# A transformer block on one core: fp8 rounding placed behind the second split, and the first batch's preparation spread over vector and scalar engine

## The reference

```
n = layernorm(x)
q, k, v = n @ qkv_w.T + qkv_b              # 16 heads of 16
o = softmax(q @ k.T / 4) @ v
x = x + o @ proj_w.T + proj_b
n = layernorm(x) ; nq = fp8_e4m3(clip(n / in_scale, -448, 448)) * in_scale
x = x + nq @ (weight_fp8 * w_scale).T + lin_bias
```

## Time and profile before

| | us |
|---|---|
| median of three runs | 1069.49 (1067.17 to 1070.72) |
| the profiled execution | 1069.94 |
| its span, first to last instruction | 1067.7 |
| TensorE busy in the span | 967.6 (91%) |
| VectorE busy | 848.5 (79%) |
| ScalarE busy | 659.4 (62%) |
| GpSimd busy | 530.0 (50%) |
| mean granted TensorE clock | 0.924 of full |

### The profile page before, as it was taken

The page is one execution under the profiler, slowest core; times in us unless marked ns, Lnnn a source line. Parts: engine busy times, 40 slices in busy tenths (PEclk is TensorE's granted clock), DMA queues, the critical chain, the costliest instruction groups (busy, mean ns, idle before and its releaser), DMA issues.

```text
span 1067.7 us, 16767 instructions
## 1 busy us (share of the span) xinstructions
PE 967.6 (91%) x5828; PEld 458.6 (43%) x5828; DVE 848.5 (79%) x1250; ACT 659.4 (62%) x1209; POOL 530.0 (50%) x533
## 2 busy tenths in 40 slices
PE   3789998989999898989989898998989899897984
PEld 2443344434444444534444443444444354433323
DVE  3678898878969787887979788897978789697616
ACT  3147776766757576766757676665667667565630
POOL 3423437384564727465463747546373845424242
PEclk9879999989989898998989899998989899899855
DMA  5971715444452444545253555535244453401010
GB/s 146 136 101 42 109 43 93 78 80 81 81 100 50 91 63 80 81 81 101 53 100 51 90 71 99 82 69 95 53 88 60 80 81 60 92 11 41 2 38 23
DMA packets 46452, 79.42 MB, mean 74 GB/s; under 512 B 10144, under 2 KB 13344, under 8 KB 46368
## 3 DMA queue, kind: packets, MB, share of 16 engines
q1 hardware_dynamic: 46368, 78.36, 42.4%
HBM read 18.42 MB, written 8.39 MB: 25 GB/s over the span
## 4 chain that ended last, share of the span: by engine, by line
PE 66%; POOL 19%; issue 7%; DVE 5%; ACT 1%; DMA 1%; SPq 0%; POOLq 0%; ACTq 0%; DVEq 0%
PE ps_t L471 20%; PE ps_o L505 18%; PE ps_s L487 6%; PE ps_m L421 5%; PE ps_m L397 5%; PE ps_m L453 4%; POOL hq L1016 3%; POOL hn L1012 3%; POOL parts L974 3%; PE ps_m L385 3%; POOL hn L996 3%; DVE mx L717 2%; POOL parts L972 2%; PE ps_m L367 1%; POOL hn L1001 1%
## 5 line engine op out<-in xcount | busy, mean ns | idle before, releaser
L595 ACT ACTIVATE pt<-ps_t 128x512 f32<-128x512 f32 x1024 | 557.7, 598 | 241.7 <-PE ps_t L471 238.4
L717 DVE TENSOR_REDUCE mx<-ps_s 128x2 f32<-128x1024 f32 x512 | 614.4, 1209 | 114.2 <-PE ps_s L487 112.1
L471 PE MATMUL ps_t<-qs,ks 50*128 50x512 f32 x1024 | 405.1, 472 | 11.2 <-ACT pt L595 11.1
L487 PE MATMUL ps_s<-ks,qs 48*128 48x512 f32 x1024 | 384.4, 469 | 6.4 <-DVE mx L717 3.3
L471 PEld LDWEIGHTS ps_t<-qs,ks 50*128 50x128 f32 x1024 | 169.0, 194 | 307.4 <-ACT pt L595 195.0
L505 PE MATMUL ps_o<-pt,vt 128*32 128x512 f32 x2048 | 290.3, 641 | 0.0
L983 POOL TENSOR_TENSOR on<-ot,rden 128x256 f32<-128x256 f32 x63 | 39.2, 622 | 280.9 <-DVE rden L778 280.9
L487 PEld LDWEIGHTS ps_s<-ks,qs 48*128 48x128 f32 x1024 | 158.8, 192 | 17.1 <-issue 7.8
L385 PE MATMUL ps_m<-xnT_p,wqkv_p 128*128 128x512 f32 x360 | 104.8, 420 | 1.2 <-POOL xnT_p L952 1.2
L974 POOL TENSOR_TENSOR parts<-parts 128x512 f32<-128x512 f32 x60 | 80.8, 1347 | 4.9
L505 PEld LDWEIGHTS ps_o<-pt,vt 128*32 128x32 f32 x2048 | 41.2, 110 | 93.7 <-issue 92.5
(11 more groups left out here) (94 smaller groups left out, 831.7 us busy)
## 6 DMA issues: line engine op xcount, KB each, us to landing
qs<-parts SPq DMA_DIRECT2D x192, 128.0 KB, 4.6
ks<-parts SPq DMA_DIRECT2D x192, 128.0 KB, 5.3
xin<-in_x SPq DMA_DIRECT2D x16, 512.0 KB, 3.6
xres<-in_x SPq DMA_DIRECT2D x16, 512.0 KB, 3.5
out<-h SPq DMA_DIRECT2D x32, 256.0 KB, 2.0
qs<-nmax SPq DMA_DIRECT2D x256, 4.0 KB
pt<-in_qkv_wT SPq DMA_DIRECT2D x1, 768.0 KB, 6.3
pt<-in_proj_wT SPq DMA_DIRECT2D x1, 256.0 KB, 5.7
```

The costliest lines, as they stand in the source:

```text
L471: nc.tensor.matmul(ps_t[:, g, :], ks[par][rows, slot, keys], qs[par][rows, slot, :], start=True, stop=True).then_inc(st_done, 1)
L487: done = nc.tensor.matmul(ps_s[:, s % 2, g, :], qs[par][rows, slot, queries], ks[par][rows, slot, :], start=True, stop=True)
L595: nc.scalar.activation(pt[n % 2][:, w % 2 + 2 * a, w // 2, :], ps_t[:, a, :], ACT.Exp, scale=SCALE).then_inc(exp_done, 1)
L717: dve.tensor_reduce(mx[:, r, :, s % QUARTER], ps_s[:, s % 2, :, :], AX_X, ALU.max).then_inc(max_done, 1)
```

## The change

GpSimd's `round_fp8(u-3)` moves from behind `split` 2 and `out_divide` 2 to right behind `split` 1. In slots without splits it thereby stands ahead of `out_divide` 2.

For batch 0, VectorE writes `xn` once `rs1` is there, and GpSimd no longer does. ScalarE, no longer VectorE, rounds the weights, ahead of its wait for the identity matrix. ScalarE makes only the rounded copies, of the transposed `xn` and of Q and K, and VectorE takes the rests straight from PSUM (for Q and K with the bias added in the same instruction).

```diff
 # scalar
                 if b == 0:
-                    nc.scalar.copy(xnT_p[:, 0, c, :], bank)
+                    nc.scalar.copy(xnT_p[:, 0, c, :], bank).then_inc(xnT_ready, 1)
+                    return
...
                 if b == 0:
-                    nc.scalar.activation(parts[:, n, 0, :].bitcast(F32R), bank, ACT.Identity, bias=bias)
+                    nc.scalar.activation(parts[:, n, 0, :].bitcast(F32R), bank, ACT.Identity,
+                                         bias=bias).then_inc(whole_ready, 1)
+                    return
...
             nc.scalar.activation(table[:], half_neg[:, 0:1], ACT.Exp)
+            act.wait_ge(w_in, 16)
+            nc.scalar.copy(wqkv_p[:, 0], wqkv).then_inc(wqkv_ready, 1)
             act.wait_ge(ident_in, 32)
 # vector, prepare()
-                dve.wait_ge(w_in, 16)
-                dve.tensor_copy(wqkv_p[:, 0], wqkv).then_inc(wqkv_ready, 1)
+                dve.wait_ge(rs1_ready, 1)
+                for j in range(NJ):
+                    last = dve.tensor_scalar(xn[:, j, :], xin[0][:, j, :], nm1[:, j:j + 1], rs1[:, j:j + 1],
+                                             ALU.add, ALU.mult)
+                last.then_inc(xn_ready, 1)
                 dve.wait_ge(wqkv_ready, 1)
                 dve.tensor_tensor(wqkv_p[:, 1], wqkv, wqkv_p[:, 0].bitcast(F32), ALU.subtract).then_inc(wqkv_ready, 1)
                 for c in range(NC):
                     dve.wait_ge(xnT_ready, c + 1)
-                    dve.tensor_tensor(xnT_p[:, 1, c, :].rearrange("p (j m) -> p j m", j=NJ), xn[:, :, c * P:(c + 1) * P],
-                                      xnT_p[:, 0, c, :].bitcast(F32).rearrange("p (j m) -> p j m", j=NJ),
+                    dve.tensor_tensor(xnT_p[:, 1, c, :], ps_t[:, c, :], xnT_p[:, 0, c, :].bitcast(F32),
                                       ALU.subtract).then_inc(xnT_low, 1)
+                dve.wait_ge(ident_in, 32)
                 for n in range(2 * NT):
                     dve.wait_ge(whole_ready, n + 1)
-                    dve.tensor_tensor(parts[:, n, 1, :], parts[:, n, 1, :], parts[:, n, 0, :],
-                                      ALU.subtract).then_inc(low_ready, 1)
+                    bias = (n % 2) * NT + n // 2
+                    dve.scalar_tensor_tensor(out=parts[:, n, 1, :], in0=ps_s[:, n // 2, n % 2, :],
+                                             scalar=b_qk[:, bias:bias + 1], in1=parts[:, n, 0, :],
+                                             op0=ALU.add, op1=ALU.subtract).then_inc(low_ready, 1)
 # gpsimd, layernorm_x
                 settled()
+                if b == 0:
+                    return
 # gpsimd, slot
                 if present(0) and u > 0:
                     split(u, 1)
+                if present(3):
+                    round_fp8(u - 3)
+                if present(0) and u > 0:
                     split(u, 2)
                 if present(2):
                     out_divide(u - 2, 2)
-                if present(3):
-                    round_fp8(u - 3)
                 if present(0) and u > 0:
                     split(u, 3)
```

## The result

The changed kernel takes 1003.85 us (median of four runs, 1002.6 to 1006.7) against 1069.2 (1067.17 to 1070.72) for the kernel before. The ratio is 0.9394, with a 95% interval of 0.9368 to 0.9419. The forecast was 1009 in a range of 999 to 1040. The profiled execution took 1006.7 us with a span of 1004.3, 63.4 less than the 1067.7 of before.

A forecast was written before the change was run, and what follows sets the result against it. TensorE was taken as the bound, stalled by late hq and slowed by the low clock behind it. Slots 58.4 us plus start 2.2 made 60.6 off the profiled 1069.94: 1009.3, said as 1009 against the median; range 999 to 1040.

The forecast's parts named there:

- The bottleneck and its price: TensorE's transposes of hq: each full slot loses 3.0 us to the stall and some 2.7 to the low clock behind it.
- hq's room: GpSimd's moved rounding: hq done at 537.71, seen by TensorE at 537.86, needed at 538.57, so 0.7 us to spare.
- What is late next: GpSimd's add_linear_bias: ends late, so TensorE stalls 1.3 us at the second linear; 4.1 us gained per slot.
- Rival A: Second linear: the new 1.3 us stall brings 1.2 GHz back; 1044 us in every slot, 1026 in half; chance 0.24.
- slot 17: Late slot without splits: only its remaining stall for hq, 1.35 us, goes.
- The start: Batch 0's preparation: projection 3.5 us earlier, 2.2 us of gain after the stacks' DMA, between 1.2 and 4.05.

The follow-up runs named there:

- e9: e3's kernel with round_fp8 and add_linear_bias both put back in the rounding's old place behind split 2 and the divide; 1065.54 us.
- e3: The changed kernel with add_linear_bias moved from behind low_oT to right behind round_fp8; 990.0 us.
- e4: The changed kernel with round_fp8 placed behind split 2 and ahead of the divide, between old and new place; 1002.81 us.
- e1: The kernel before with only the move of round_fp8 behind split 1, the start unchanged; 1006.31 us.
- e8: The changed kernel with xn of batch 0 written by GpSimd again; 1004.7 us (one run).
- e5: e3's kernel with two more clips of hn, which change no value, ahead of the rounding; 1015.88 us (two runs).
- e2: The changed kernel with round_fp8 put back behind split 2 and the divide, leaving the start alone changed; 1066.4 us.
- e7: e3's kernel with the load of x of batch 2 issued behind the first batch's stacks of pieces 0 and 1; 990.4 us (one run).
- e10: e3's kernel with four more clips of hn, which change no value, ahead of the rounding; 1066.0 us (one run).
- e6: e3's kernel with three more clips of hn, which change no value, ahead of the rounding; 1039.26 us (two runs).

## Why the prediction was right, point by point

**The bottleneck and its price.** Forecast: 3.0 us of stall and 2.7 us of low clock per slot, removed by the move. e9 against e3 gives 61.4 - 55.95 = 5.45 per slot, of which 3.02 is stall and 2.4 clock. Right, the clock's share 0.3 too large. The reason is the full-clock time from the transposes to the second linear: summed up as 6.5 us, it is 6.81 in e3 (226.07 to 232.88), and 9.15 - 6.81 = 2.34.

**hq's room.** Forecast 0.86 us from the end of L1016 (537.71) to TensorE's need (538.57), 0.7 with the hand-over taken off; measured 0.73 from the end of L1028 to the transposes.

**What is late next.** Forecast: the bias, a stall of 1.3 us at the second linear, 4.1 us net per slot. Measured: 1.26, 1.21 in the slot shown, and 61.45 - 57.33 = 4.12. e4 and e3 show that this chain, not hq or VectorE, is what is left. VectorE's reductions behind L824 were in time.

**Rival A, the clock.** It came true in 2 of 13 slots, not in none. The slot in which it is plainest, and the stretch behind it:

```profile
464.65 1.97 PE L453 MATMUL ps_m<-wlin_p,hqT 128*128 128x256 f32 x8 [1.53 <-DVE h L824]
```

```profile
464.60:471.40 6.80, 6.75 (x38) 4.37 (x40) 6.53 (x13) 2.32 (x5) 4.38 (x7) 0.75 0.37 123
```

Its stall was the longest, 1.53, because GpSimd's chain ran 0.3 us late in this one slot; the other, slot 3, had 1.40. But a stall of 1.30 was also followed by a fall (e1, slot 8, clock 0.75 in the same stretch), one of 1.40 in e1's slot 3 was not, and in e8, which has the same order in its slots, thirteen stalls of 1.25 to 1.34 brought no fall at all. What decides is not shown. A slot with a fall was 1.7 us longer, not 2.7, 0.1 to 0.3 of it the longer wait: the low clock lasted for about half of the 6.8 us of the earlier trace rows. Two of these, 3.3 us, are the shortfall of 49.2 against 46.24.
The Trainium skill, in TensorE: Matmul & The Clock Gate, on PSUM-queue depth-cycling, describes a clock that swings with frequent short idles. The traces agree for two slots of thirteen in the changed kernel (waits of 1.40 and 1.53 us) and six of thirteen in e5 (1.56), and disagree for e8 and for e4, where waits of 1.3 us, or of 1.0 and 0.2, brought no fall.

**The step that failed: slot 17.** Forecast 1.35 us, measured 6.38. The stall at L436 went as said. The missing 5.0 us are clock. From second linear to second linear TensorE does the same 257 matmuls and is idle for 58.89 - 51.34 = 7.55 us before and 52.51 - 46.38 = 6.13 after; the other 4.96 us are busy time, at a granted clock of 0.77 and 0.90:

```profile
978.70:1037.59 58.89, 51.34 (x257) 19.00 (x255) 28.34 (x45) 34.50 (x63) 21.18 (x18) 0.77 0.06 20
```

```profile
921.70:974.21 52.51, 46.38 (x257) 18.55 (x255) 28.32 (x45) 34.27 (x63) 21.12 (x18) 0.90 0.07 22
```

In the earlier trace rows the clock fell at about 1008, early in slot 17; after, behind stalls of the same 0.74 us, it held until about 963:

```profile
951.15 0.99 PE L471 MATMUL ps_t<-qs,ks 50*128 50x512 f32 x2 [0.74 <-ACT pt L595]
...
963.66 1.28 PE L471 MATMUL ps_t<-qs,ks 50*128 50x512 f32 x2 [0.74 <-ACT pt L595]
```

```profile
951.00:963.60 12.60, 9.72 (x48) 2.90 (x48) 4.11 (x14) 9.19 (x19) 9.58 (x10) 0.98 0.01 2
```

It is no property of the change: e1, with the same orders in slot 17, has 0.63 for the same stretch of 951.00 to 963.60, and needed 56.89 us from second linear to second linear. That is 2.0 less than before at nearly the same clock (0.79), and this is what the forecast's 1.35 priced. Over the same piece the clock was 0.79 in e1, e2, e3, e7 and e9, 0.90 in the changed kernel, e4, e5, e8 and e10, and 1.00 in e6, whose slot took 49.66 us. So the clock of this thin slot comes out differently, worth 4 us or more, where TensorE's work in it is the same; what decides is open. The changed kernel's own runs spread over 4 us. The forecast gave the clock's part no term at all. The term should have been a range instead of a value: by these runs 2.0 (e1) to 6.8 us (e4, with 52.06).

**The start.** Forecast: projection 3.5 us earlier, 2.2 of it coming through a DMA-paced stack, bounds 1.2 and 4.05. Measured 2.8 (the weights landed 1 us later than before in this execution; 3.4 to 3.5 in e2, e3 and e4) and 37.01 - 34.84 = 2.17. The chain was forecast rightly, weights, ScalarE's rounding, VectorE's subtraction, two rests: 4.9 us from the weights' arrival (8.3 to 13.2), measured 4.52, with the weights 1 us later than assumed. That 2.17 hits 2.2 is partly luck: seven other versions with this start gained 0.6 (e3) to 2.8 (e6). By slot 3's L436, whose scores ended at 171.20 before and at 167.97 now, 3.2 us were saved in the changed kernel's profile, 1.0 in e2's, and 1.6 in e1's, which has the old start. So executions differ there by as much as the start is worth. The DMA rate in the stacks' stretch was different: 126 GB/s before, 153 after, 127 in e3, 136 in e2. Why it differs between executions is open.

```profile
24.00:36.00 12.00, 6.81 (x33) 5.35 (x31) 6.78 (x22) 3.44 (x6) 2.05 (x3) 0.86 1.08 126
```

```profile
24.00:34.00 10.00, 5.01 (x27) 4.12 (x25) 4.61 (x16) 1.17 (x2) 3.17 (x5) 0.83 1.07 153
```

(Stretches of the start, the kernel before and the changed one.) Part of the changed kernel's 5.84 us in the first piece is thus one execution's luck; slot 3 itself gave 5.84 - 3.23 = 2.6, against 2.8 forecast.

In sum the slots were 3.1 us worse than forecast, slot 17 was 5.0 better and the start 0.8 better; 60.6 became 63.4, and the median of the changed kernel lies 2.9 below the profiled execution's own time, which is the other half of the 5 us between 1009 and 1003.85.

## What to carry to other kernels

When a stall is removed, follow the engine that was late to the next thing it hands over: here the work moved out of the way stood in front of a bias add that nobody had waited for before, and it cost 1.3 us of the 5.4 that could be had; moving that too gave another 14 us. Price a stall of TensorE with the slower matmuls behind it, which nearly doubled it here, and give a thin stretch, in which the clock came out differently from run to run, a range. A gain in the start of a pipeline is worth only what the next wait, here a DMA, lets through.

## What the runs showed that was not expected

The clock's price does not grow steadily with the stall. In the profiled executions it is nothing at 1.0 us, nothing in most slots and 1.2 to 1.6 in the others at 1.3 to 1.6, 1.1 in nearly all at 2.66, 2.0 to 2.5 at 3.02 to 3.04, and 2.6 falling to 1.7 at 3.76. e6 and e10 missed their expectations for this. Slots with stalls of 3.02, 3.04 and 3.76 us end up at the same distance, 61.4: e9's get there from 61.0, e10's from 62.3. In the last slots of e10 TensorE stood idle for 0.7 us more than in e9 at no cost. Why the distances settle is not shown.

GpSimd's four instructions of 128x256 took 4.36 us beside VectorE's rounding and subtraction of the weights, and 2.16 with neither beside them (e8). The Trainium skill, in GPSIMD Engine Reference, Key points, says that GpSimd contends with VectorE in two-port modes and with two SBUF inputs. The trace agrees for the subtraction, which has two inputs (2.05 us for 0.55); that the copy ran in a two-port mode (1.24 for 0.55) no run here shows.
